# One attention and expert block on one core: the prologue put in another order

## The reference, cut to what matters

```python
# x: (8, 512, 128), 16 heads of 64, 32 frequencies, 16 experts with a hidden size of 512
mod = (silu(c) @ wmod).reshape(8, 6, 1, -1); sa, ca, ga, sb, cb, gb = six rows of mod
ga, gb = sign(ga) * max(|ga|, 0.25), sign(gb) * max(|gb|, 0.25)
h = layernorm(x) * (1 + ca) + sa
q, k, v = einsum('bsx,xAnh->Abnsh', h, w); q = q + q_bias
a = (q k^T + relative_causal(q emb^T)) / 8          # emb = sins @ positional, per head
o = softmax(causal(a)) v
x = x + ga * (o @ out_kernel + out_bias)
h = layernorm(x) * (1 + cb) + sb
score = softmax(h @ Wg + bg); idx = argmax(score)   # 256 places per expert, late tokens dropped
x = x + gb * score[idx] * (relu(h @ W1[idx] + b1[idx]) @ W2[idx] + b2[idx])
```

## Time and profile before

| what | value |
|---|---|
| median of 3 runs | 910.6 us (909.8 to 910.83) |
| profiled execution, its own time | 910.37 us |
| its span, first to last instruction | 908.6 us |
| mean granted clock of TensorE | 0.982 |
| busy: TensorE / VectorE / ScalarE / GpSimd | 97% / 73% / 78% / 57% |
| chain that ended last: TensorE's share | 90% |

### The profile page before, as it was taken

One profiled execution on the slowest core, in us unless ns is written; L12 is line 12 of the kernel. 1 busy time (PEld: TensorE's weight loads), 2 busy tenths in 40 slices (PEclk: granted clock), 3 DMA queues, 4 the chain that ended last, 5 costly groups with the idle time before them and its releaser, 6 DMA issues.

```text
span 908.6 us, 17567 instructions
## 1 busy us (share of the span) xinstructions
PE 878.4 (97%) x5594; PEld 702.5 (77%) x5594; DVE 663.6 (73%) x2052; ACT 710.9 (78%) x1968; POOL 517.4 (57%) x782
## 2 busy tenths in 40 slices
PE   6999999999999999999999999999999999998994
PEld 4777778777778787777787777777877777766994
DVE  4677678786878778777878787868777777752884
ACT  3788888888888888888888888888888888841541
POOL 2454555666556755675556556575567555633354
PEclk7799999999999999999999999999999999999998
DMA  7000960001000000000000000000000000006661
GB/s 278 2 1 7 272 164 13 1 1 37 13 1 1 36 1 14 1 18 17 13 2 15 12 13 1 1 21 1 13 1 21 1 13 2 9 18 220 216 211 39
DMA packets 23068, 39.12 MB, mean 43 GB/s; under 512 B 3094, under 2 KB 16135, under 8 KB 22592
## 3 DMA queue, kind: packets, MB, share of 16 engines
q1 hardware_dynamic: 19184, 29.30, 10.8%
q0 software_dynamic: 3072, 5.94, 1.8%
q10 hardware_dynamic: 720, 2.75, 0.9%
HBM read 23.63 MB, written 16.82 MB: 45 GB/s over the span
## 4 chain that ended last, share of the span: by engine, by line
PE 90%; POOL 1%; issue 1%; DVE 1%; ACT 1%; POOLq 0%; DVEq 0%
PE bank L748 22%; PE bank L778 16%; PE bank L713 16%; PE bank L758 15%; PE bank L785 5%; PE bank L734 5%; PE bank L745 3%; PE bank L948 3%; PE bank L937 2%; PE bank L902 2%; PE bank L806 1%; POOL out L439 1%; PE bank L793 0%; PE bank L800 0%; PE bank L928 0%
## 5 line engine op out<-in xcount | busy, mean ns | idle before, releaser
L395 POOL TENSOR_SCALAR prob<-prob,rsum 128x128 f32<-128x128 f32 (+3 forms) x512 | 263.2, 532 | 243.9 <-DVE rsum L1074 238.2
L538 ACT ACTIVATE prob<-srow,nmax 128x512 f32<-128x512 f32 (+3 forms) x512 | 286.4, 560 | 69.1 <-DVE nmax L1062 66.4
L1062 DVE CUSTOM_DVE_ANT_0 srow<-bank,consts 128x512 f32<-128x512 f32 (+3 forms) x512 | 246.9, 489 | 100.6 <-issue 77.8
L758 PE MATMUL bank<-consts,prob 128*128 128x128 f32 x1280 | 201.8, 272 | 0.5 <-ACT pt L547 0.2
L758 PEld LDWEIGHTS bank<-consts,prob 128*128 128x128 f32 x1280 | 158.3, 140 | 23.5 <-ACT pt L547 1.1
L388 POOL TENSOR_TENSOR qlo<-qx,qhi 128x384 fp32r<-128x384 f32 x128 | 129.6, 1012 | 51.8 <-ACT qhi L514 50.9
L547 ACT ACTIVATE pt<-bank 128x384 f32<-128x384 f32 x318 | 153.3, 495 | 5.4 <-PE bank L758 5.3
L778 PE MATMUL bank<-pt,v 128*64 128x512 f32 (+3 forms) x1024 | 152.0, 439 | 0.2 <-issue 0.2
L748 PE MATMUL bank<-khi,qhi 128*128 128x512 f32 (+2 forms) x384 | 146.6, 382 | 4.0 <-DVE klo L1085 1.6
L1079 DVE SCALAR_TENSOR_TENSOR qx<-bank,qbias,consts 128x512 f32<-128x512 f32 x128 | 94.1, 736 | 52.9 <-PE bank L713 52.9
L748 PE MATMUL bank<-khi,qlo 128*128 128x512 f32 (+2 forms) x384 | 130.8, 341 | 0.0
(11 more groups left out here) (167 smaller groups left out, 1415.7 us busy)
## 6 DMA issues: line engine op xcount, KB each, us to landing
xbuf<-fill SPq DMA_DIRECT2D x4, 1540.0 KB, 23.9
x<-xbuf SPq DMA_DIRECT2D x16, 385.0 KB
raw<-in_w SPq DMA_DIRECT2D x16, 256.0 KB, 11.8
prob<-in_w SPq DMA_DIRECT2D x16, 256.0 KB, 2.9
out<-row SPq DMA_DIRECT2D x8, 256.0 KB, 2.5
x<-in_x SPq DMA_DIRECT2D x1, 1792.0 KB, 14.3
modb<-mod_rows SPq DMA_DIRECT2D x1, 1536.0 KB, 8.6
v<-in_b SPq DMA_DIRECT2D x1, 1024.0 KB, 7.2
```

Source lines behind the costliest of these rows:

```text
L395: end = gp.tensor_scalar(part, part, rsum[:, par, 4 * h + q:4 * h + q + 1], 1.0, ALU.mult, ALU.mult)
L538: act.activation(prob[:, par, h, QOFF[q]:QOFF[q] + P * (q + 1)], srow[:, k % 4, 0:P * (q + 1)], ACT.Exp, bias=nmax[:, par, k:k + 1], scale ...
L758: last = pe.transpose(out[:, n * P:(n + 1) * P], prob[:, par, h, QOFF[q] + k * P:QOFF[q] + (k + 1) * P], ident)
L1062: dve.tensor_tensor_reduce(out=srow[:, k % 4, 0:w], in0=scb[k % 2][:, 0:w], in1=mask[:, S - w:S], scale=-1.0, scalar=BIG, op0=ALU.add, op1 ...
```

## The change

1. The three loads of the rotation table move from SP's queue to ScalarE's, behind the weights of pair 0; their copies on ScalarE (khi) move ahead of hn. The zero part of the mask is no longer loaded but set by GpSimd (`open`).
2. The split of the weights is cut in two: pairs 1 to 3 in the prologue, now after the evacuation of the first queries on VectorE; pairs 4 to 7 in step 1 (`second_step` on ScalarE, slots 6 and 7 on VectorE, and GpSimd in step 2). `high_wo` moves from slot 2 to slot 1 of step 1. TensorE waits for the second part in step 3, slot 4.
3. On TensorE the 8 idle matmuls become 36, 16 more stand behind L701; the W tables of pairs 1 to 3 move behind the first queries, and the bias products and the W tables of pairs 4 to 7 move out of step 0, ahead of its scores.
4. `modulation` is cut into five pieces, in steps 3, 4 and 5.

```diff
-            sp.dma_start(consts[:, 128:], consts_d[:, 128:]).then_inc(s["consts"], 16)
-            sp.dma_start(h2T[HD:P, :], ktab_d).then_inc(s["ktab"], 16)
-            for h in range(2):
-                sp.dma_start(kx[HD:P, h, :], ktab_d[:, 0:P]).then_inc(s["ktab"], 16)
+            sp.dma_start(consts[:, 512:], consts_d[:, 128:]).then_inc(s["consts"], 16)
...
+            gp.memset(consts[:, 128:512], 0.0).then_inc(s["open"], 1)
...
+                    if first and a == 2:
+                        low_wk(4, PAIRS, 8)
...
-            low_wk()
+            low_wk(1, 4, 3)
...
             act.dma_start(wall[:, 0:1, :], wall_d[:, 0:1, :]).then_inc(s["wall0"], 16)
+            act.dma_start(h2T[HD:P, :], ktab_d).then_inc(s["ktab"], 16)
+            for h in range(2):
+                act.dma_start(kx[HD:P, h, :], ktab_d[:, 0:P]).then_inc(s["ktab"], 16)
...
+            def second_step(k):
+
+                if k == 1:
+                    high_wo()
+                if k == 2:
+                    high_wq(4, PAIRS, 0)
+                if k == 3:
+                    high_wq(4, PAIRS, 1)
+                if k == 4:
+                    high_wk(4, PAIRS)
...
-                    if first and (a, k) == (1, 2):
-                        high_wo()
+                    if first and a == 1:
+                        second_step(k)
...
-            idle(8)
+            idle(36)
...
-            pe.wait_ge(s["wall1"], 16)
-            w_table(1, 4)
+            idle(16)
...
-                if k == 1:
-                    pe.wait_ge(s["wall2"], 16)
-                    b_table(1, PAIRS)
-                if k == 2:
-                    w_table(4, PAIRS)
...
+                    if k == 4 and a == 3 and first:
+                        pe.wait_ge(s["whi"], 8)
+                        pe.wait_ge(s["wlo"], 6)
+                        pe.wait_ge(s["wlo_k"], 2)
...
+            pe.wait_ge(s["wall1"], 16)
+            w_table(1, 4)
             project_k(0, None, 0)
+            pe.wait_ge(s["wall2"], 16)
+            b_table(1, PAIRS)
+            w_table(4, PAIRS)
...
             low(0)
-            for h in range(2):
-                low_wq(h)
...
+                    if first and (a, k) in ((1, 6), (1, 7)):
+                        low_wq(4, PAIRS, k - 6, k)
...
-                    elif (a, k) == (4, 5):
-                        modulation()
+                    elif (a, k) in ((3, 5), (3, 6), (4, 5), (4, 6), (5, 5)):
+                        modulation(2 * a + k - 11)
...
             evac_q(0, 0, 0)
             evac_q(0, 0, 1)
+            for h in range(2):
+                low_wq(1, 4, h, h + 1)
             low_k(0, 0)
```

More of the change, by code:

```diff
@@ L174, in program @@
         mod_dram = nc.dram_tensor("mod_rows", [B, 3 * D], F32).ap()
-        names = ("ident consts small wall0 wall1 wall2 w_v ktab x0 x1 wmod misc b2 wo zero "
+        names = ("ident consts open small wall0 wall1 wall2 w_v ktab x0 x1 wmod misc b2 wo zero "
                  "e_silu silu wg_mm bias fhi flo whi wlo wlo_k mod_mm modT mev mrow modb gates "
@@ L286, in turn @@
                     sp.wait_ge(s["flo"], 3)
-                    sp.wait_ge(s["wlo_k"], 1)
-                    sp.wait_ge(s["wlo"], 4)
+                    sp.wait_ge(s["wlo_k"], 2)
+                    sp.wait_ge(s["wlo"], 6)
                     sp.wait_ge(s["wv"], 2)
@@ L342, in low_table, with low_wk @@
                 gp.wait_ge(s["kt"], 4)
[L344 to L349, removed]
+            def low_wk(a0, a1, after):
+                gp.wait_ge(s["whi"], after)
+                gp.tensor_tensor(wlo[:, a0:a1, 2 * P:3 * P], wall[:, a0:a1, P:2 * P], whi[:, a0:a1, 2 * P:3 * P],
+                                 ALU.subtract).then_inc(s["wlo_k"], 1)
             def copy(n, i):
@@ L600, in step, with high_wq, high_wk @@
                     evac_o(j - 1)
+            act.wait_ge(s["ktab"], 48)
+            for h in range(2):
+                act.activation(khi[HD:P, h, :], h2T[HD:P, :], ACT.Copy).then_inc(s["kt"], 1)
+            def high_wq(a0, a1, h):
+                act.activation(whi[q_cols(a0, a1, h)], wall[q_raw(a0, a1, h)], ACT.Copy).then_inc(s["whi"], 1)
+            def high_wk(a0, a1):
+                act.activation(whi[:, a0:a1, 2 * P:3 * P], wall[:, a0:a1, P:2 * P], ACT.Copy).then_inc(s["whi"], 1)
             act.wait_ge(s["modT"], 2)
@@ L604, in _ @@
             high(0)
-            act.wait_ge(s["ktab"], 48)
-            for h in range(2):
-                act.activation(khi[HD:P, h, :], h2T[HD:P, :], ACT.Copy).then_inc(s["kt"], 1)
             act.wait_ge(s["wall1"], 16)
[L609 to L612, removed]
+            high_wq(1, 4, 0)
+            high_wq(1, 4, 1)
+            high_wk(1, 4)
             high_q(0, 0)
@@ L1020, in low_wv, with low_wq @@
                 dve.tensor_tensor(wvlo[:, :], wv, wvhi[:, :], ALU.subtract).then_inc(s["wv"], 1)
[L1022 to L1026, removed]
+            def low_wq(a0, a1, h, after):
+                dve.wait_ge(s["whi"], after)
+                dve.tensor_tensor(wlo[q_cols(a0, a1, h)], wall[q_raw(a0, a1, h)], whi[q_cols(a0, a1, h)],
                                   ALU.subtract).then_inc(s["wlo"], 1)
@@ L1175, in index, with modulation @@
                     .then_inc(s["idx"], 1)
-            def modulation():
-                dve.wait_ge(s["mev"], 1)
-                dve.tensor_copy(upper16[:, :], upper).then_inc(s["zero"], 1)
-                link(dve.tensor_scalar(mrow[:, 1, :], mrow[:, 1, :], 1.0, None, ALU.add))
-                for g_, sign, size in ((modT[:, 4, :], gtmp[:, 0, :], gtmp[:, 1, :]),
-                                       (mrow[:, 2, :], mtmp[:, 0, :], mtmp[:, 1, :])):
+            def modulation(i):
+                if i == 0:
+                    dve.wait_ge(s["mev"], 1)
+                    dve.tensor_copy(upper16[:, :], upper).then_inc(s["zero"], 1)
+                    link(dve.tensor_scalar(mrow[:, 1, :], mrow[:, 1, :], 1.0, None, ALU.add))
+                    return
+                g_, sign, size = ((modT[:, 4, :], gtmp[:, 0, :], gtmp[:, 1, :]),
+                                  (mrow[:, 2, :], mtmp[:, 0, :], mtmp[:, 1, :]))[(i - 1) // 2]
+                if i % 2:
                     link(dve.tensor_scalar(sign, g_, 0.0, 2.0, ALU.is_ge, ALU.mult))
                     link(dve.scalar_tensor_tensor(size, sign, -1.0, g_, ALU.add, ALU.mult))
+                else:
                     link(dve.tensor_scalar(size, size, 0.25, None, ALU.max))
@@ L1369, in host_constants @@
     causal = np.where(np.arange(P)[None, :] > np.arange(P)[:, None], NEG, 0.0)
-    mask = np.concatenate([np.zeros((P, S - P)), causal], axis=1)
     desc = np.broadcast_to(E - np.arange(E), (P, E))
@@ L1373, in host_constants @@
     token = (np.arange(P)[:, None] + P * np.arange(TILES)[None, :]).astype(np.float64)
-    consts = np.concatenate([np.eye(P), mask, qtab, desc, upper, token], axis=1)
+    consts = np.concatenate([np.eye(P), causal, qtab, desc, upper, token], axis=1)
     return np.ascontiguousarray(consts, dtype=np.float32), np.ascontiguousarray(ktab, dtype=np.float32)
```

3 lines of the change are left out of this document (added).

## The result

The changed kernel takes **907.58 us** (median of 6 runs, 906.4 to 908.34) against 910.8 (6 runs, 909.8 to 911.03) on the same chip: ratio 0.9965, 95% interval 0.9952 to 0.9977. So 3.2 us are gained (2.1 to 4.4), where 5.7 were forecast. The profiled execution took 908.34 us, the longest of the six, with a span of 906.5 (before 908.6) and a mean granted clock of 0.994 (0.982). The agreement of sign and range hides misses of opposite sign.

The account below looks back on a forecast made before the run. Three limits in turn were taken to bound the head: the chain to the first scores, a slow PE, then DVE with ACT; later PE. Gains 4.2 + 0.5 + 1.0 = 5.7 off 910.4, plus 0.2, gave 904.9 us; range 902.2 to 909.2.

Parts of the forecast that it names:

- Nothing: Rival: ACT's later start eats what the queries gain, step 0 stays at 14.6 us: 910 us; chance 0.06.
- Part 1: Head, up to the first scores: these come at 21.0 us, 2.1 us earlier; bounds 20.0 and 25.2.
- The tables ending right before the scores: Sign in the head: first scores near 21 us, with PE's W tables ending right before them.
- Part 2: Step 0: ACT bounds, 11.42 us of work plus 1.9 of waits; step 1's first exponential comes 13.3 us later.
- The half-clock rivals: PE at half clock until the first scores (908.9 us, chance 0.10) or through step 0 (915.5 us, chance 0.06).
- Part 3: Step 1: PE uses 0.8 us of wohi's vanished wait; subtractions (0.6 to 1.6) stick out 0.2; 0.5 us gained.
- Part 4: Gates: modulation in five pieces over steps 3 to 5 is hidden, PE's hole goes; 1.0 us gained, at least 0.

Follow-up runs that it names:

- a_idle8: Changed kernel with 8 idle matmuls instead of 36 ahead of the transposes: 904.09 us, ratio 0.9935 to the kernel before.
- a_tables_sp: Changed kernel with the rotation table's three loads back on SP's queue, behind the identity: 905.41 us, ratio 0.9949 to the kernel before.
- a_both: Changed kernel with tables on SP's queue and 8 idle matmuls, khi's copies still ahead of hn: 905.96 us, ratio 0.9964 to the kernel before.
- a_products: Changed kernel with the bias products and W tables of pairs 4 to 7 back in step 0: 906.03 us, ratio 0.9958 to the kernel before.
- b_tables_act: Kernel before with only the rotation table's three loads moved to ScalarE's queue: 911.86 us, ratio 1.0016 to the kernel before.
- b_gates: Kernel before with only the modulation cut into five pieces: 908.65 us, ratio 0.9989 to the kernel before.
- best8: Changed kernel with tables on SP's queue, 8 idle matmuls, khi's copies behind the split of pairs 1 to 3: 903.56 us, ratio 0.9914 to the kernel before.
- a_gates_whole: Changed kernel with the modulation in one piece again, step 4, slot 5: 907.1 us, ratio 0.9971 to the kernel before.

## Why the prediction was right, and where not

The sign and the range were right; the number was 2.7 us too good. That the time fell into the range is in part luck: the head gave 2.8 us less than forecast, step 0 1.1 more. The rival "Nothing" had the head right (ACT's later start eats what the queries gain) and step 0 wrong. By its own steps, in us gained in the profiled execution:

| step | forecast | measured |
|---|---|---|
| to step 0's first exponential | 2.9 | 0.1 |
| step 0 | 1.3 | 2.4 |
| step 1 | 0.5 | 0.6 |
| the gates, at step 4 | 1.0 | 1.26 |
| drift to 808 us | 0 | -1.05 |

- **Part 1 failed** at the sentence "L688, ahead of them, waits for silu and moves by some 0.9 us". Its twin L711 moved by 3.1, from 6.34 to 9.48, as it waited for `wmod`, which is issued behind the tables, and not for silu; and it ran at half rate, 2.27 us instead of 1.25. The idle matmuls so started at 11.60 instead of the forecast 8.3. That is the step at fault, and the sum had followed x alone. In x's path the size was a little off as well: "the path of x loses 0.6 to 1.4 us. I take 1.0" became 1.49 at the statistics, the table load having moved by 2.2 (3.25 to 5.46). But xn, ready at 11.56, was not what the transposes waited for.
- The second fault of Part 1 was the end of the idle matmuls, "between 11.0 and 12.3". The upper price was right (4.02 us for 36, 4.00 here); with the later start they ended at 15.60, and the transposes came at 15.40 instead of 11.6. Eight of them let the transposes start 2.9 us sooner (a_idle8). In the forecast they already held them by 0.5. Work that only keeps the clock must end before the real work is ready, also when something ahead of it slips.
- The tables: landed before the wait for the transposes, as assumed, on ACT's queue. The Trainium skill ("DMA: Bandwidth & Descriptors", Queues, rings and completion order) says that each DMA engine goes round between the queues; by that rule the tables would have had 224 KB of their own queue ahead on ACT's, and 368 KB (columns, x, identity) on SP's in a_tables_sp and a_both. The traces agree in which comes first, 4.2 to 5.5 us on ACT's queue and 7.2 to 8.3 on SP's, where the tables hold hn in a_both; the difference is larger than these kilobytes make it: 144 KB more would be 0.9 us even at 169 GB/s, the mean of the changed kernel's first 5 us (an estimate).
- From vlo's end on Part 1 was 1.0 us too slow: 4.98 us to the scores (18.72 to 23.70), forecast 6.0 (15.0 to 21.0). Most of that is the bias products, 1.05 us here; their 1.66 was read in a stretch at half clock. "The tables ending right before the scores" was right too; that their move out of step 0 pays no run shows (a_products).
- **Part 2 was better than forecast**: 12.13 us against 13.3. ACT works 11.02 of 12.20 and waits 1.2, where the forecast kept 1.9; full clock held from 17.54 on. The half-clock rivals are refuted by the window, 1.00 through step 0.
- **Part 3 held** within 0.1 us (its own terms, 0.8 less 0.2, make 0.6 and not 0.5). The two subtractions cost 0.42 and 1.22, together the 1.6 of the upper bound, for the reason given: the second runs beside GpSimd.
- **Part 4 held at its place** and not in the total: "1.0 us gained" was 1.26 at step 4, and 1.05 were lost again by 808 us. Nothing in the prediction stands for that loss. Most of it is the meeting of DVE and GpSimd in the seventh steps, which also strikes a kernel whose gates are whole (b_tables_act), so the trace does not charge it to the cut; by time the cut is worth 1.0 us (b_gates, 0.2 to 1.8).
- Between 808 us and the end the profiled execution loses another 1.3 us of its lead (3.36 to the 2.1 between the spans). PE waits there for a DMA for which it does not wait in the kernel before, the gather of the experts' rows, as the list of PE's waits over 110 to 900 us has it (engine, line, waited for: us, times, longest):

```profile
PE bank L954 <- DMA x<-xbuf: 1.1, 1, 1.1
```

best8 and b_gates wait for that DMA too. What brings it there was not tried and stays open; the medians, 3.2 us apart, agree with the lead at 808 us rather than with the end of this one execution.

## What to carry to other kernels

In these kernels a DMA issue on a compute engine's queue was paid twice: by that engine's first instruction, and by every load that now stood behind it; follow each of them to whoever waits for it, not only the path that one meant to shorten. Filler work that keeps TensorE's clock belongs into a wait only as far as the wait is sure to last, and a copy whose load may be late belongs behind the work of the path. A hole that is closed in one step can lose its worth again in later ones: measure the lead at the end too, and before the loss is charged to the edit, look whether a kernel without that edit loses the same.

## What was not expected of the hardware

- The record of the granted clock can mislead at its start. The windows of the changed kernel and of a_gates_whole over the idle matmuls (11.6 to 15.3 us), same instructions, one fence for each:

```profile
11.60:15.30 3.70, 3.70 (x37) 3.70 (x38) 0.58 (x4) 0.00 (x0) 2.50 (x2) 1.00 1.01 431
```

```profile
11.60:15.30 3.70, 3.70 (x36) 3.70 (x36) 0.71 (x5) 0.00 (x0) 2.49 (x2) 0.50 1.02 435
```

  One says 1.00, the other 0.50, and both took the same time for 36 matmuls (4.00 and 3.89 us, some 110 ns each). The first recorded change of the clock in the changed kernel is at 17.54; ahead of it the record shows 1.00 whatever the rate. So part of the rise of the mean clock from 0.982 to 0.994 is of the record, and durations decide: 16 idle matmuls took 1.07 us at full (17.68) and, in best8, 1.89 at half (12.43).
- The same subtraction on DVE took 0.42 us by itself and 1.22 beside a subtraction of GpSimd (46.44 and 47.50 above); vlo took 0.69, 0.86 and 1.62 us by how much of it lay beside klo (changed kernel, a_tables_sp, a_both). An operation on four columns took 0.17 us or 1.02 in the same place of the program (192.15 above). A move that puts such work next to GpSimd's costs up to the difference.
- The tables landed 7.2 to 8.3 us after their issue on SP's queue behind 368 KB, 9.8 to 10.3 behind 968 KB (before and b_gates), and 4.2 to 5.5 us on ACT's queue behind 224 KB. It is not the queue alone: the 64 KB of the identity, just ahead of them on SP's queue, landed after 4.1 to 4.8.
